# Value products of two key blocks issued together, every second block, in both attentions of a two-layer network

## What is computed

```python
# layer 0 (B): x (2, 1024, 512), q, k, v: (2, 32, 1024, 16)
scores = jnp.einsum('bhqd,bhkd->bhqk', q, k) / jnp.sqrt(16.)
out = jnp.einsum('bhqk,bhkd->bhqd', jax.nn.softmax(scores, axis=-1), v)
# layer 1 (G): k, v: (2, 1024, 16), shared by the heads
scores = jnp.einsum('bqhd,bkd->bhqk', q, k) * scale
scores = jnp.where(causal[None, None], scores + alibi[None], -1e30)
attn = jnp.einsum('bhqk,bkd->bqhd', jax.nn.softmax(scores, axis=-1), v)
```

## Time and profile before

| | us |
|---|---|
| median of 3 runs | 2366.48 |
| span of the profiled execution | 2362.2 |
| TensorE busy in it | 2131.0 (90%) |
| VectorE busy in it | 1474.3 (62%) |
| ScalarE busy in it | 1157.6 (49%) |
| first attention, from about 204 to 977 | 773 |
| second attention, from about 1586 to 2149 | 563 |

### The profile page before, as it was taken

One profiled execution on the slowest core, in us unless ns is written; L12 is line 12 of the kernel. 1 busy time (PEld: TensorE's weight loads), 2 busy tenths in 40 slices (PEclk: granted clock), 3 DMA queues, 4 the chain that ended last, 5 costly groups with the idle time before them and its releaser, 6 DMA issues. The chain is left out here.

```text
span 2362.2 us, 38051 instructions
## 1 busy us (share of the span) xinstructions
PE 2131.0 (90%) x12048; PEld 1101.9 (47%) x12048; DVE 1474.3 (62%) x2004; ACT 1157.6 (49%) x2387; POOL 287.1 (12%) x476
## 2 busy tenths in 40 slices
PE   7987999999999999787999996769999999998685
PEld 5761222222222222375888785634434443445564
DVE  5317887887878887274433232637767676764677
ACT  4321776776767777513322221425656565564153
POOL 1220010101001001030000000121111111111203
PEclk9995999999999999997999998879999999999888
DMA  5343422242223420125010101331111011101411
GB/s 176 121 134 43 60 35 33 33 58 38 33 33 47 49 33 5 54 101 167 24 36 1 36 18 39 126 95 33 28 41 40 21 40 40 27 16 55 145 66 71
DMA packets 124485, 132.92 MB, mean 56 GB/s; under 512 B 36422, under 2 KB 88454, under 8 KB 124336
## 3 DMA queue, kind: packets, MB, share of 16 engines
q1 hardware_dynamic: 122880, 129.31, 23.0%
q10 hardware_dynamic: 1296, 1.28, 0.3%
q0 software_dynamic: 160, 0.15, 0.0%
HBM read 89.71 MB, written 40.17 MB: 55 GB/s over the span
## 5 line engine op out<-in xcount | busy, mean ns | idle before, releaser
L735 DVE TENSOR_REDUCE maxesB<-s_psB 128x1 f32<-128x1024 f32 x512 | 603.3, 1220 | 158.8 <-PE s_psB L773 158.3
L719 ACT ACTIVATE probsB<-st_psB 128x512 f32<-128x512 f32 x1024 | 529.0, 602 | 210.2 <-PE st_psB L813 208.6
L735 DVE TENSOR_REDUCE maxesG<-s_psG 128x1 f32<-128x896 f32 (+7 forms) x512 | 364.6, 754 | 174.8 <-PE s_psG L776 170.9
L719 ACT ACTIVATE probsG<-st_psG 128x512 f32<-128x512 f32 (+3 forms) x768 | 325.8, 491 | 217.9 <-PE st_psG L816 157.1
L773 PE MATMUL s_psB<-k_stackB,q_stackB 96*128 96x512 bf16 x1024 | 320.7, 396 | 22.2 <-DMA k_stackB<-k_parts 17.7
L813 PE MATMUL st_psB<-q_stackB,k_stackB 99*128 99x512 bf16 x1024 | 325.0, 386 | 11.0 <-issue 6.9
L796 PE MATMUL o_psB<-probsB,v_onesB 128*32 128x512 f32 x2048 | 275.5, 606 | 0.3 <-issue 0.2
L773 PE MATMUL s_psG<-k_stackG,q_stackG 105*128 105x512 bf16 (+3 forms) x768 | 208.3, 341 | 32.9 <-DMA q_stackG<-in_bias_q 15.9
L813 PEld LDWEIGHTS st_psB<-q_stackB,k_stackB 99*128 99x128 bf16 x1024 | 78.5, 97 | 337.8 <-ACT probsB L719 280.5
L813 PE MATMUL st_psG<-q_stackG,k_stackG 108*128 108x512 bf16 (+3 forms) x768 | 215.7, 334 | 15.2 <-issue 9.3
L796 PE MATMUL o_psG<-probsG,v_onesG 128*32 128x512 f32 (+3 forms) x1536 | 164.1, 500 | 0.0
(11 more groups left out here) (252 smaller groups left out, 3063.8 us busy)
## 6 DMA issues: line engine op xcount, KB each, us to landing
q_stackB<-q_parts SPq DMA_DIRECT2D x186, 64.0 KB
k_stackB<-k_parts SPq DMA_DIRECT2D x93, 128.0 KB
q_stackG<-q_parts SPq DMA_DIRECT2D x186, 64.0 KB
q_parts<-partsA SPq DMA_DIRECT2D x16, 384.0 KB, 2.5
k_parts<-partsA SPq DMA_DIRECT2D x16, 384.0 KB, 2.5
q_parts<-partsF SPq DMA_DIRECT2D x16, 384.0 KB, 2.6
xA<-in_x SPq DMA_DIRECT2D x4, 1024.0 KB
v_rows<-voutA SPq DMA_DIRECT2D x16, 256.0 KB, 3.3
```

The costliest lines, as they stand in the source:

```text
L719: act.activation(probs[:, (i % ring) * GH + h, first:HALF], st_ps[:, bank_of(n), first:HALF], ACT.Exp).then_inc(st_used, 1)
L735: dve.reduce_max(maxes[:, half, h * QT + qt:h * QT + qt + 1], s_ps[:, n % 2, 0:key_width(half, qt)], AX.X).then_inc(maxed, 1)
```

## The change

The value products of steps i-2 and i-1 are issued one behind the other at every even step i; odd steps issue none. At step 0 the last two of the iteration before are issued, and the last two of all behind the last body.

```diff
--- before.py
+++ after.py
@@ -821,8 +821,10 @@
                                 row_scores(it + 1, (buf + 1) % 3, *unit)
                             units = units[spacing:]
                     if i == 0 and before:
+                        values(it - 1, n_steps - 2)
                         values(it - 1, n_steps - 1)
-                    if i > 0:
+                    if i > 0 and i % 2 == 0:
+                        values(it, i - 2)
                         values(it, i - 1)
                     if i == turn_at[half] and not (last and half == 1):
                         n = where[("max", half, 0)]
@@ -838,6 +840,7 @@
                 if half == 0:
                     turn_max(0, 0, 2)
             run(pe, body)
+            values(ITS - 1, n_steps - 2)
             values(ITS - 1, n_steps - 1)
```

## The result

The changed kernel takes **2377.84 us** (median of 4 runs, 2375.92 to 2381.15) against 2366.58 us of the kernel before in the same comparison (4 runs): **+11.3 us**, ratio 1.0051, 95% interval 1.0039 to 1.0062. The forecast was 2378.4 us, +11.9.

What follows compares the result with a forecast made beforehand. TensorE's order of issue was taken to set the step, with VectorE's slack only 0.55 us in 2.91. Terms +12.6 + 2.6 - 1.1 - 2.2 = +11.9 us on 2366.5 gave 2378.4 us, range 2364 to 2390 us.

Steps and rivals of the forecast that it cites:

- What bounds the kernel, and the drains: TensorE's issue order sets the 2.91 us step; fewer passages between bf16 and narrow fp32 products save 0.18 us per pair.
- The walk through a pair: First attention: even step's second unit waits for VectorE's maximum until 3.49; pair 5.92 us against 5.82, +0.10.
- what would show it: Signs listed beforehand: first-attention pair of 5.9 us, gap of 0.15 to 0.2 us before the even step's second unit.
- Turn: First-attention pairs with a turn: it stands alone behind a unit, adding 0.39 to 0.40 us; pair 6.13 against 6.02.
- The last iteration: First attention's last iteration, without units: ScalarE's three banks don't cover the gap, +0.45 us per pair, +2.6 us in all.
- The return of the loop: TensorE's stall at the loop's return, four times per attention: VectorE and ScalarE work off backlog, -1.1 us.
- The second attention: Pair 9-10 loses 0.32 us, other pairs gain or stay: -0.14 us an iteration, x 16 = -2.2 us.
- The sum: Whole kernel: all terms added, +11.9 us, to 2378.4 us.
- The median and the span: Span of before, 2362.2 us, lies 4.3 us under the median; this difference was held constant.
- The first (only the drains count): Rival for both attentions: 224 pairs keep 0.18 us, -40 us, turns give back 6; 2332 us, chance 0.08.
- The third (two calls pay the passage too): Rival: second value call follows the first at 0.54 us rather than 0.46, +20 us, 2398 us; chance 0.07.
- The second (the second attention returns what the first loses): Rival: second attention's pairs except 9-10 keep 0.18 us, some half-clock stretches go; 2368 us, chance 0.15.

Runs made afterwards that it cites:

- e5: Kernel before, with VectorE taking the first attention's row maximum over the first 512 of 1024 keys only: 2355.53 us, ratio 0.9949.
- e6: Changed kernel, with VectorE taking the first attention's row maximum over the first 512 of 1024 keys only: 2359.25 us, ratio 0.9967.
- e7: Changed kernel, with the last iteration of both attentions issuing its value products singly: 2373.3 us, ratio 1.0024.
- e3: Changed kernel, with the pair spanning two iterations (last step and step 0) taken apart in both attentions: 2373.7 us, ratio 1.0033.
- e2: Kernel before, with value products paired in the second attention only: 2362.63 us, ratio 0.9984.
- e4: Kernel before, with second attention paired only at steps 2, 4, 6 and 8, singly in its last iteration: 2355.5 us, ratio 0.9953.
- e8: Second attention paired only at steps 2, 4, 6, 8, their last row-score unit moved behind the two value calls; against kernel before: 2348.46 us, ratio 0.9924.
- e1: Kernel before, with value products paired in the first attention only: 2382.0 us, ratio 1.0065.

## Why the prediction was right, point by point

**What bounds the kernel, and the drains.** Right. TensorE's order sets the step; e5 took half of VectorE's work away and no steady step moved. The second call follows the first without a passage, as rows 6 suggested: the steps are 0.45, 0.43, 0.43 and 0.55 us. I had taken 0.46 for the first three. That term was mis-sized by 0.05 us a pair: the two calls take 1.86 instead of 1.91 us, so what a pair saves is 0.23 us and not 0.18.

**The walk through a pair.** Right in place and nearly in size. Forecast: odd step 1.82, second unit at 3.49 because of VectorE, pair 5.92. Measured: 1.82, 3.48, 5.88. The two calls' 0.05 is nearly all of the difference. The wait stands at the second unit of the even step, as named in what would show it, and e6 took it away and got 5.72 us, where the walk without it gives 3.31 + 0.52 + 1.91 = 5.74. The steady iteration therefore cost +0.61 instead of +0.84 us, 9.2 instead of 12.6 us in all. *Turn*: 0.41 us, forecast 0.40; the pair with a turn 6.10 us, forecast 6.13.

**The last iteration.** The pair was walked to 5.24 us and takes 5.22 (959.49 to 964.71 in the trace's starts of key scores), but the sum was short: +4.0 instead of +2.6. The seven pairs cost 2.9 us (walked: 3.1). The 0.5 us taken off at the end weren't there (the last step is 3.02 us in both kernels), and step 0, which closes the pair begun in the iteration before, takes 1.07 us more; I hadn't counted it to this iteration. In the second attention I had counted the last iteration at -0.14 like any other, and it costs +3.3 us. In e7's expectation I put that down to ScalarE. The first part of it is another term, which the prediction set at nothing ("the maxima's rows start at the same steps"): TensorE waits 1.75 us for these rows instead of 0.59, so step 4 starts 1.1 us later, and 3.4 us at half clock follow. The run with the unit behind has such a stretch with single calls, and its last iteration takes 1.6 us more than the 25.8 of the others, 0.2 of them a longer wait. By these numbers, an estimate, 1.1 of the 3.3 us are the wait and 1.4 the clock, and some 0.8 are left for the pairs. The first transfer takes 2.8 us to land instead of 1.7; why, stays open.

**The return of the loop.** Wrong in sign, the step of the prediction that failed. It said -1.1 us, since VectorE and ScalarE would work off their backlog in the stall. That is small beside what I hadn't asked: what had covered the branch. Value products queued in front of it did, for 1.0 us, and the change moved them behind it. The loop also returns three times and not four: its last branch falls through, in 0.08 us. Measured +4.6 and +3.0 us; e3 gave back 4.1 and 2.2 of it. The +4.6 is a comparison of two single profiles, and about 1 us of it is chance. With the first attention in its old order the returns cost 10.8 us (before), 11.4 (e2), 12.1 (e4) and 13.3 (e8), and in the new order 15.4, 14.6 (e1) and 16.4 (e7): in the mean +3.6.

**The second attention.** The walked pair is right almost to the digit: units at 2.43 and 3.56 us (forecast 2.43 and 3.56), value products 0.60 later, pair 5.80 us (5.85), +0.28 (+0.32). The pairs that I only estimated gained more: 1-2 0.30, 3-4 0.25, 5-6 0.04, 7-8 0.23, 11-0 0.02 us, so -0.56 us an iteration, at the lower bound of -0.58 and not at -0.14. They gained more than 0.18 us because of the same term as above: a pair saves 0.23 us, which is what 3-4 and 7-8 show. Pair 1-2 has besides 0.06 us less of waits in front of its units (0.65 instead of 0.71).

**The sum** came out at +11.3 for +11.9 because these errors cancel, which is luck. Against the forecast: steady first attention -3.4, its last iteration +1.4, steady second attention -6.3 (-8.4 against -2.1 for 15 iterations), its last +3.4, returns +5.7 and +3.0. Of +11.9 as forecast and the +14.9 of the two profiled spans, the working was right only in the pairs that were walked step by step, and the total is better than its parts.

**The median and the span.** I held the 4.3 us between span and median constant. The lowest run of before, 2364.37 us, is 2.2 us above the span, and the profiled run of after (2379.09 us) 2.0 us above its span of 2377.1. So some 2 us lie around the span, and the rest was that the profiled run of before was a fast one. In medians the change is 11.3 us, between the profiles 14.9.

**The rivals.** The first (only the drains count) is excluded by the pair of 5.88 us. Its rule, the Trainium skill's from "TensorEngine Tiling (Array Packing)", "Key Properties", isn't: the drains are there and are saved. The third (two calls pay the passage too) is excluded by the 0.43 us between two calls' products. The second (the second attention returns what the first loses) had the right mechanism for the second attention, -8.4 us in the steady part, and was outweighed by the returns and the last iterations, which it didn't name. Its other half came out the other way: there was more half clock and not less.

## What to carry to other kernels

Grouping work of a kind on the bounding engine shortens its own list, but every buffer between it and the others must hold the longer gap: walk one period from the starts in the trace, and look which engine with little slack (here 0.55 us in 2.91) is asked for more between two groups. Walk each kind of stage by itself, the last iteration and the loop's return too, since they had other limits than the steady part and their 14.9 us are here as much as the whole difference of the spans (the steady parts, +9.2 and -8.4, nearly cancel). Then group only where it gains, and move the piece that waits behind the group: that made -0.8% out of a change of +0.5%.

## What the runs showed of the hardware

- A loop's return costs TensorE's sequencer 3.3 to 3.8 us in this kernel, with one call of value products queued or none (3.6 to 4.1 with two in the first attention; 4.8 to 5.1 in one variant, unexplained). In the first attention work on the array in front of it covers 1.0 us with one call, and only 1.2 us with two (1.9 us of work).
- Behind a return the granted clock often falls to half (1.2 GHz) for 3.4 or 6.8 us. How often differed between kernels whose first attention is the same: 3.4 us in all before, 6.8 with only the second attention in pairs, 10.2 with the set 2, 4, 6, 8 and again 10.2 with the unit behind. The changed kernel and the runs e1 and e7, with the same pairs in the first attention's loop, had 13.6 each, but so had e5 in the old order. I can't attribute these stretches to the change. Half of the 6.8 us between 3.4 and 10.2, so up to 3.4 us, is what they can make of one profile against another of the same code (an estimate). A window of the changed kernel behind its first return (length, busy time of PE, PEld, DVE, ACT and POOL, clock, DMA share, GB/s):

```profile
415.70:422.50 6.80, 6.35 (x24) 1.61 (x24) 2.45 (x2) 2.17 (x4) 0.00 (x0) 0.50 0.01 2
```

- Value products and the turn, both fp32 and narrow, follow each other with no passage; each change between them and full-width bf16 products costs 0.09 us (turn behind value products 0.43 us in rows 6, as far apart as value products in a pair).
- The wait for the maximum's rows in the last iteration of the second attention (0.59 us before, 1.75 after) was followed by 3.4 us at half clock in the four traces with 1.50 to 1.75 us of it, and in one of the eight with 0.41 to 0.80 us (the one with 0.80).
